# An expert layer's token weights moved to the inner rows, and an attention's keys and values projected for two groups at once

## The chip, the cores and the metric

The kernel runs on one core of a Trainium2 chip. The metric is the device time of one execution in microseconds (us); the number to compare is the median of three runs. Engines are named as in the profile: PE is TensorE, DVE is VectorE, ACT is ScalarE, POOL is GpSimd, SP is SyncE, which here only issues DMAs.

## The reference, cut to what matters

Four transformer layers follow each other, each with an attention part and an expert part. Only two of the eight parts are touched: layer 0's attention and layer 0's experts. In the kernel there are 16 batches of 256 tokens, 128 channels, all float32.

```python
# layer 0, attention: 64 query heads of 64, 8 key/value heads (each serves a group of 8 query heads)
q = (x @ Wq.T + bq); k = (x @ Wk.T + bk); v = (x @ Wv.T + bv)      # k, v repeated 8 times
allowed = (qi >= kj) & (qi - kj < 128)
logits = concat([where(allowed, q k^T * scale, -1e30), sink]); o = softmax(logits)[..., :-1] @ v
return o @ Wo.T + bo

# layer 0, experts: H = 128, M = 64, 16 experts, top 4 of 16 within the best 2 of 4 groups
scores = sigmoid(x @ gate_kernel) + gate_bias
combine = top4_weights(scores) * 2.5 / sum                          # n x 16, zero where not chosen
inter = silu(x @ w_gate[e]) * (x @ w_up[e])                         # n x 64 for each expert
y = sum_e combine[:, e] * (inter @ w_down[e])
shared = (silu(x @ sw_gate) * (x @ sw_up)) @ sw_down                # inner width 128
return y + shared
```

## The kernel before, in words

Every engine runs its own hand-written instruction stream; the streams meet in counting semaphores. `past(e, sig, v)` and `e.wait_ge(...)` are waits, `.then_inc` counts up. Parts follow each other in the order in which `program` lists them. SP loads the weights of later parts when their buffers come free.

**First attention** (`attention_plan`, `attention_pe`, `attention_dve`). The work is cut into 128 groups (16 batches times 8 key/value heads), each of two units of four query heads. A round handles unit `i`; rounds alternate even and odd. PE in each round computes `scores(i)` (L406), `values` of the unit four rounds back (L444), the transposes of the unit three rounds back (L169); an even round adds the projection step `q0` (L389) of the next group, the output projection `out` (L430) and the step `kv` of the next group (keys L382, values L384); an odd round adds `q1` (L389). The projections share one PSUM bank, `a.side`; semaphore `free` says that DVE or ACT has emptied it. For `kv` DVE runs one `tensor_scalar` for the keys (L497) and one `tensor_tensor` for the values (L500). The key weights are stored twice side by side, so that the 64 key rows of a group lie on partitions 0 to 63 and again on 64 to 127: the even heads multiply on the one half, the odd heads on the other. DVE in each round merges and masks the scores (L509, L521), writes transposed weights (L532), and computes shifts and inverses (L542 to L557). PE may write the next scores only when DVE has masked the last ones.

**First expert layer** (`moe_plan`, `moe_pe`, `moe_act`, `moe_dve`, `moe_pool`). PE computes the gate's logits during the layer norm before it. DVE then ranks the experts (`gate_groups_dve`, `rank`, L1065 to L1155) and writes `f.comb`, one weight for each token and expert. PE, ACT and DVE wait for it before the first unit. The tokens are cut into 8 blocks of 512; each block takes 9 units: 8 pairs of experts (two inner widths of 64 fill the 128 partitions) and the shared expert. In a unit PE runs two 512-column multiplications (L1205, L1207), ACT the silu (L1246), DVE the product (L1272), PE four output multiplications (L1230), and DVE multiplies the outputs by the token's weight and adds them to `f.acc` in SBUF (L1309). For a pair, the output of the two experts must stay apart, because their weights differ: the right-hand side is 256 columns wide (each half zero in the other expert's rows), and DVE runs 8 multiply-adds of 128 x 128; for the shared expert it is 128 columns and 4. At a block's end POOL multiplies by the gate row and adds to `k.X`, and DVE takes the statistics for the next layer norm. `moe_*` also serves layer 2's experts, with 16 units a block and its own code paths (`l == 2`).

Of the kernel before, what the change touches and what calls it, by code (L numbers as in the profile page):

```python
# [127 lines left out]
def setup(nc, ctx, dram, out):  # L128
# [9 lines left out]
    k.hrow = nc.dram_tensor("hrow_dram", (NB * 256, 256), F32, kind="Internal").ap()  # L138
    sb = lambda n, w: ctx.enter_context(nc.sbuf_tensor(n, [P, w], F32))
# [183 lines left out]
def attention_plan(k, l, no, w, t_w):  # L323
# [6 lines left out]
    a.qT, a.kT = R.many(2, 1024), R.many(2, 256)  # L330
    a.nv = 4
    a.va = G.many(a.nv, 128)
# [10 lines left out]
    a.uses = {("q0", 0): 0, ("kv", 0): 1, ("q1", 0): 2}  # L343
    for n in range(1, a.groups):
        for part in ("q0", "kv", "q1"):
            a.uses[part, n] = len(a.uses)
    u = a.units
    a.s = sems(k, "a", zero=2, part=2, early=u, half=3 * u, merged=2 * u, masked=3 * u, shift=u, sshift=u, exps=u, sexp=u, inv=u, norm=2 * u, turn=2 * u,
# [21 lines left out]
def attention_pe(k, a, e):  # L370
# [6 lines left out]
    def project(step, n):  # L377
# [15 lines left out]
    def scores(i):  # L393
# [3 lines left out]
        q, kt = a.qT[n % 2], a.kT[n % 2]  # L397
        e.wait_ge(*s["free"](max(taken(f"q{s4}", n), taken("kv", n))))
        past(e, s["masked"], 3 * i)
        for p, qt, j, last in ((0, 0, 0, 0), (1, 1, 0, 0), (0, 0, 1, 0), (0, 1, 0, 0), (1, 1, 1, 1), (0, 1, 1, 1),  # L400
# [5 lines left out]
            m = e.matmul(o, q[r, 256 * c + 128 * qt:256 * c + 128 * qt + 128], kt[r, 0:w_], start=True, stop=True)  # L406
# [27 lines left out]
    def values(i):  # L434
        if i is None:
            return
        v, pt = a.va[i // 2 % a.nv], a.PT[i % 2]
        past(e, s["o"], i)
        for c in range(3):
# [3 lines left out]
            for r in range(2):  # L443
                done(e.matmul(a.Ob[64 * r:64 * r + 64, at:at + 256], v[:, 64 * tile:64 * tile + 64], x[:, r],  # L444
                              start=(c != 1), stop=(c != 0)), s["values"], c == 2 and r == 1)
# [3 lines left out]
    for i, at, odd, ahead, n in attention_rounds(a):  # L449
# [14 lines left out]
        else:  # L464
# [6 lines left out]
            if ahead is not None:  # L471
                project("kv", ahead)


def attention_dve(k, a, e):
# [7 lines left out]
    e.tensor_tensor(a.isnew, k.C["ident"], k.C["tri"], ALU.add).then_inc(s["part"].sem, 1)  # L483
    c_.hold(e)
    e.wait_ge(*s["part"](2))
    e.wait_ge(*s["zero"](2))

    def project(step, n):
# [7 lines left out]
        else:  # L496
            e.tensor_scalar(a.kT[n % 2], a.side[:, 0:256], w["bk"][:, g:g + 1], None, ALU.add)  # L497
            past(e, s["values"], 2 * (n + 1 - a.nv))
            bv = w["bv"][:, 64 * g:64 * g + 64].unsqueeze(1).broadcast_to([P, 2, 64])
            e.tensor_tensor(a.va[n % a.nv].rearrange("p (t w) -> p t w", t=2),  # L500
                            a.side[:, 256:384].rearrange("p (t w) -> p t w", t=2), bv, ALU.add).then_inc(s["free"].sem, 1)
# [59 lines left out]
    for i, at, odd, ahead, n in attention_rounds(a):  # L561
# [25 lines left out]
        else:  # L587
# [6 lines left out]
            if ahead is not None:  # L594
                project("kv", ahead)
# [464 lines left out]
def rank(c, q, vals, n, C, out):  # L1060

    C4 = C.rearrange("p (t e j) -> p t e j", e=n, j=n)
    for e in range(n):
        if e:
# [3 lines left out]
                               ALU.is_gt))  # L1068
    c.hold(q)
# [19 lines left out]
def gate_groups_plan(k, f, r, spare):  # L1089
    nc_ = 17 if f.l == 0 else 16  # L1090
    f.comb = v3(r.get(NT * nc_), nc_)
    n0 = r.at
    f.g = spare.get(512), spare.get(512), r.get(128), r.get(128), r.get(512), r.get(512), r.get(32), r.get(8192)
    r.at = n0
# [7 lines left out]
def gate_groups_dve(k, f, q):  # L1102
# [35 lines left out]
    rank(c, q, m3, 16, C, rk3)  # L1138
# [14 lines left out]
    if l == 0:  # L1153
        c.then(q.memset(f.comb[:, :, 16:17], 1.0))
    q.tensor_tensor(f.comb[:, :, 0:16], w3_, bc(den, 16), ALU.mult).then_inc(f.s["comb"].sem, 1)  # L1155

# [4 lines left out]
def moe_plan(k, l, no, gate, t_w, r):  # L1161
    f = K()
    f.l, f.no, f.gate, f.t_w = l, no, gate, t_w
    f.w = views(k.W2, {0: L0F, 2: L2F}[l])
    spare = k.W2[:, width(L0F):width(L2F)] if l == 0 else k.W1[:, width(L3F):width(L1F)]
    gate_groups_plan(k, f, r, Region(spare, spare.shape[1]))
    f.sg, f.h, f.acc, f.ym = r.many(3, 512), r.many(3, 512), r.many(2, 512), r.many(2, 512)
    if l == 0:
        f.yb, f.E = [(k.bank[4], k.bank[5]), (k.bank[6], k.bank[7])], 9
    else:  # L1170
        f.yb, f.E = [(k.bank[4],), (k.bank[5],), (k.bank[6],)], 16
    f.cT = r.get(4096) if l == 2 else None
    u = 8 * f.E
    totals = dict(logits=1, gexp=1, comb=1, gated=u, lifted=u, silu=u, hidden=u, half={0: 64, 2: 8}[l], down=u,
                  sum=u + (8 if l == 2 else 0), scaled=24, tox=8)
    if l == 2:
        totals |= dict(ct=8, ctp=8)
    f.s = sems(k, "f", **totals)
# [4 lines left out]
def moe_pe(k, f, e):  # L1183
# [6 lines left out]
    if l == 2:  # L1190
        for g in range(8):
            past(e, s["ct"], g - 1)
            for j in range(4):
                done(transpose(k, e, k.bank[4 + g % 2][0:16, 128 * j:128 * j + 128], f.comb[:, 4 * g + j, :]), s["ctp"],
                     j == 3)
    for u in range(8 * E + 1):
        if u < 8 * E:
            B, x_e = divmod(u, E)
            x = k.HT[:, 512 * B:512 * B + 512]
            if l == 0 and x_e == 8:  # L1200
                w1, w3 = w["sw1"], w["sw3"]
            else:
                w1, w3 = w["w1"][:, 128 * x_e:128 * x_e + 128], w["w3"][:, 128 * x_e:128 * x_e + 128]
# [46 lines left out]
def moe_dve(k, f, e):  # L1250
# [10 lines left out]
    for u in range(8 * E + 1):  # L1261
# [11 lines left out]
        if u >= 1:  # L1273
# [11 lines left out]
            for q in range(2 if two else 1):  # L1285
                for j in range(4):
# [12 lines left out]
                    else:  # L1299
                        src = ys[0][:, 128 * j:128 * j + 128]  # L1300
                        if j == 0:
                            e.wait_ge(*s["down"](d + 1))
# [1432 lines left out]
```

## Time and profile before

| | |
|---|---|
| median of 3 runs | 4342.83 us (4336.99 to 4345.63) |
| the profiled execution's own time | 4335.0 us |
| its span, first to last instruction | 4333.2 us |
| TensorE clock granted, mean | 0.931 |
| busy: PE, DVE, ACT, POOL | 90%, 76%, 51%, 30% |
| DMA, mean over the span | 11 GB/s |
| first attention | from about 48 to 1640 us |
| first expert layer | from about 1657 to 1954 us |

Busy shares are means over stages with different limits. A busy PE is not PE at its peak: its records overlap, so what a step costs is read from the distance between the starts of neighbouring records. A float32 multiplication shows as two records, a transpose as one.

### The profile page before, as it was taken

The numbers are of one execution on the slowest core, as the hardware profiler recorded it, in microseconds if no ns is written. First come the engines' busy times: TensorE is split into PE (matmuls) and PEld (weight loads), VectorE is DVE, ScalarE is ACT, GpSimd is POOL, SyncE is SP. The second block draws the span as 40 slices with busy tenths as digits, with TensorE's granted clock in tenths as the row PEclk, the third lists the DMA queues.
The fourth block names the chain that finished last, engine by engine and source line by source line (L and its number), as shares of the span: only waits on it lengthen the run. The fifth ranks groups of instructions, "written<-read, shape, count | busy, mean of one in ns | idle before, by whom it ended". The sixth has DMA issues, their size and how long they took to land.

```text
span 4333.2 us, 78923 instructions
## 1 busy us (share of the span) xinstructions
PE 3898.3 (90%) x25405; PEld 2636.7 (61%) x25405; DVE 3302.3 (76%) x12175; ACT 2220.0 (51%) x6877; POOL 1297.2 (30%) x1077
## 2 busy tenths in 40 slices
PE   6999999999999996998998996998975999899835
PEld 5777777777777775665664443334553666555633
DVE  6888888888888886884776996776887777788561
ACT  4777777777777772114675443433222222477501
POOL 1333333333333330003453884550000000222107
PEclk9999999999999997996998998999985999999857
DMA  2000000000000002000000000000001000000103
GB/s 116 2 2 2 2 2 2 2 2 2 1 2 2 2 2 85 1 1 1 2 2 1 0 0 10 1 1 1 1 1 59 1 1 1 1 2 1 40 24 54
DMA packets 20344, 46.59 MB, mean 11 GB/s; under 512 B 1248, under 2 KB 17632, under 8 KB 18656
## 3 DMA queue, kind: packets, MB, share of 16 engines
q1 hardware_dynamic: 13792, 35.25, 2.1%
q0 software_dynamic: 6144, 6.30, 0.9%
q8 instruction: 208, 3.41, 0.3%
q14 instruction: 200, 1.64, 0.1%
HBM read 33.15 MB, written 8.39 MB: 10 GB/s over the span
## 4 chain that ended last, share of the span: by engine, by line
PE 70%; DVE 15%; issue 6%; ACT 5%; POOL 3%; DMA 1%; POOLq 0%; DVEq 0%; ACTq 0%; SPq 0%
PE ps L406 9%; PE ps L444 9%; PE ps L169 8%; PE ps L389 6%; PE ps L430 5%; PE ps L1230 5%; PE ps L1205 4%; PE ps L1207 3%; PE ps L1803 2%; PE ps L1790 2%; DVE gbbc L1842 2%; PE ps L833 2%; DVE gbbc L1837 2%; DVE gbbc L1831 2%; PE ps L797 2%
## 5 line engine op out<-in xcount | busy, mean ns | idle before, releaser
L521 DVE CUSTOM_DVE_ANT_0 T<-ps,C 128x128 f32<-128x128 f32 x2048 | 450.7, 285 | 0.0
L668 POOL TENSOR_TENSOR T<-T 128x512 f32<-128x512 f32 x256 | 260.8, 1039 | 535.2 <-DVE T L557 535.2
L668 POOL TENSOR_TENSOR W<-W,T 128x512 f32<-128x512 f32 x256 | 260.8, 1040 | 520.8 <-DVE T L557 520.8
L406 PE MATMUL ps<-T 64*128 64x128 f32 (+1 forms) x4096 | 404.7, 337 | 1.7 <-DVE T L521 1.7
L532 DVE COPY_PREDICATED W<-gbbc,ps 128x512 f32<-128x512 int32 x512 | 342.7, 722 | 82.2 <-PE ps L169 82.2
L615 ACT ACTIVATE W<-T 128x128 f32<-128x128 f32 x1024 | 396.1, 391 | 1.7 <-DVE T L542 1.7
L615 ACT ACTIVATE T<-T 128x128 f32<-128x128 f32 x1024 | 396.1, 391 | 0.5 <-DVE T L542 0.5
L444 PE MATMUL ps<-W,gbbc 128*64 128x256 f32 x3072 | 388.0, 388 | 2.7 <-ACT T L632 2.7
L406 PEld LDWEIGHTS ps<-T 64*128 64x128 f32 x4096 | 343.9, 187 | 62.9 <-issue 42.5
L169 PE MATMUL ps<-C,T 128*128 128x128 f32 (+1 forms) x1649 | 277.9, 308 | 95.0 <-DVE T L292 44.9
L169 PEld LDWEIGHTS ps<-C,T 128*128 128x128 f32 (+1 forms) x1649 | 205.5, 153 | 170.3 <-issue 63.0
L1230 PEld LDWEIGHTS ps<-W,T 128*128 128x128 f32 x1600 | 238.1, 191 | 115.8 <-issue 103.8
L1309 DVE SCALAR_TENSOR_TENSOR T<-ps,T 128x128 f32<-128x128 f32 x1024 | 286.5, 343 | 27.1 <-PE ps L1230 11.1
L389 PE MATMUL ps<-HT,W 128*128 128x256 f32 x1024 | 277.6, 394 | 2.0 <-ACT HT L315 1.1
L1230 PE MATMUL ps<-W,T 128*128 128x128 f32 (+1 forms) x1600 | 266.2, 309 | 9.0 <-DVE T L1272 5.6
L983 ACT ACTIVATE T<-ps 128x384 f32<-128x384 f32 (+1 forms) x512 | 236.0, 550 | 71.1 <-PE ps L784 71.0
L444 PEld LDWEIGHTS ps<-W,gbbc 128*64 128x64 f32 x3072 | 197.7, 136 | 108.4 <-ACT T L632 3.5
L1333 POOL TENSOR_TENSOR T<-T,gbbc 128x256 f32<-128x256 f32 x32 | 23.2, 724 | 783.5 <-DVE T L1309 783.5
L1041 POOL TENSOR_TENSOR QK<-T,QK 128x512 fp32r<-128x512 f32 x128 | 162.0, 1275 | 311.3 <-ACT T L1004 227.9
L509 DVE COPY_PREDICATED ps<-C,ps 128x256 f32<-128x256 int32 x512 | 199.3, 425 | 65.6 <-PE ps L406 65.1
L624 ACT ACTIVATE W<-ps 128x512 f32<-128x512 f32 x256 | 152.8, 597 | 186.8 <-PE ps L169 182.5
L430 PE MATMUL ps<-T,W 128*128 128x256 f32 x1024 | 242.3, 379 | 0.8 <-ACT T L632 0.8
(375 smaller groups left out, 8852.1 us busy)
## 6 DMA issues: line engine op xcount, KB each, us to landing
W<-in_l1f_dram SPq DMA_DIRECT2D x1, 6152.0 KB, 24.5
W<-in_l0a_dram SPq DMA_DIRECT2D x1, 5172.5 KB, 24.5
W<-in_l2f_dram SPq DMA_DIRECT2D x1, 3160.0 KB, 11.4
W<-in_l3f_dram SPq DMA_DIRECT2D x1, 3076.0 KB, 18.4
W<-in_sm_dram SPq DMA_DIRECT2D x1, 2729.0 KB, 9.6
W<-in_l0f_dram SPq DMA_DIRECT2D x1, 2256.0 KB, 29.4
X<-in_x_dram SPq DMA_DIRECT2D x1, 2048.0 KB, 12.7
out_dram<-X SPq DMA_DIRECT2D x1, 2048.0 KB, 8.7
```

The lines of the kernel that those rows point to most:

```text
L169: return e.transpose(out, in_, k.C["ident"])
L389: done(e.matmul(a.side[:, 256 * c:256 * c + 256], w["wq"][:, 512 * g + 128 * (2 * j + c):512 * g + 128 * (2 * j + c) + 128], x, start=True ...
L406: m = e.matmul(o, q[r, 256 * c + 128 * qt:256 * c + 128 * qt + 128], kt[r, 0:w_], start=True, stop=True)
L430: done(e.matmul(a.acc[:, 0:256], w["wo"][:, (g * a.CH + c) * 128:(g * a.CH + c + 1) * 128], a.oT[n % 2][:, 256 * c:256 * c + 256], start=( ...
L444: done(e.matmul(a.Ob[64 * r:64 * r + 64, at:at + 256], v[:, 64 * tile:64 * tile + 64], x[:, r], start=(c != 1), stop=(c != 0)), s["values" ...
L521: done(e.tensor_tensor_reduce(sm[:, at:at + 128], src, m, 1.0, -3.0e38, ALU.add, ALU.max, mx[:, col:col + 1]), s["masked"], x == (3 if ban ...
L532: e.copy_predicated(a.PT[t % 2][:, 512 * j:512 * j + 512].rearrange("p (h w) -> p h w", h=4), is_.unsqueeze(1).broadcast_to([P, 4, 128]).b ...
L615: done(e.activation(a.Pr[i % 4][:, at:at + w_], a.Sm[i % 2][:, at:at + w_], ACT.Exp, bias=a.ngs[i % 4][:, c:c + 1], scale=a.scale, accum_o ...
L668: e.tensor_tensor(pr, pr, a.rins[i % 4][:, c:c + 4].unsqueeze(2).broadcast_to([P, 4, 128]), ALU.mult).then_inc(s["norm"].sem, 1)
L983: e.activation(a.PT[n % 2][:, 512 * g:512 * g + 256 + a.w1], a.far[g][:, 0:256 + a.w1], ACT.Exp, bias=0.0, scale=a.scale).then_inc(s["exp" ...
L1230: m = e.matmul(o, hh[:, 128 * j:128 * j + 128], rhs, start=True, stop=True)
L1309: m = e.scalar_tensor_tensor(out=a, in0=src, scalar=c, in1=a, op0=ALU.mult, op1=ALU.add)
```

## The change

It has three parts, in layer 0 alone except where said.

1. **Attention, keys and values.** The `kv` step runs once for two groups. Because the key weights lie twice side by side, 128 columns taken from an offset of 64 give group g's keys on partitions 0 to 63 and group g+1's on 64 to 127. DVE adds the bias (two small copies at the part's start build `a.bk`), then copies the two halves crosswise into columns 256 to 511. The values multiplication has 128 columns where it had 64. `scores` waits for a semaphore of its own, `keys`.
2. **Experts.** New functions `fold_*` replace `moe_*` for layer 0. The token's weight multiplies the inner rows `h` before the output multiplication, and so the two experts of a pair need not stay apart: `fold_pool` adds their two zero-padded weight blocks once, the right-hand side is 128 columns wide, and all nine units of a block accumulate in one PSUM bank. The weights are needed along the columns of `h`: PE transposes `f.comb` (4 transposes for a block), ACT copies them to SBUF, SP writes them to DRAM (`crow`) and reads them back with each row broadcast over 64 partitions, two DMAs of 128 KB for a unit into one of three buffers `cB`. DVE multiplies (`scale`). The output multiplications lag five units behind (`FOLD_LAG`), and the first six units run while DVE still ranks (`between`). At a block's end DVE does what POOL did.
3. **Ranking, both expert layers with groups.** The comparison table `C` is bf16 where it was float32, in half the space. `moe_*` loses its layer 0 paths.

```diff
@@ attention_plan
+    a.qT, a.kT = R.many(2, 1024), R.many(2, 512)      # kT was 256
+    a.nv = 3                                          # was 4
+    a.va = G.many(a.nv, 256)                          # was 128
@@ attention_pe, project("kv") and scores
-            e.matmul(a.side[:, 0:256], w["wk"][:, 128 * g:128 * g + 128], x, start=True, stop=True)
+            e.matmul(a.side[:, 0:256], w["wk"][:, 128 * g + 64:128 * g + 192], x, start=True, stop=True)
             for j in range(2):
-                done(e.matmul(a.side[:, 256 + 64 * j:320 + 64 * j], x[:, 128 * j:128 * j + 128],
-                              w["wv"][:, 64 * g:64 * g + 64], start=True, stop=True), s["side"], j == 1)
+                done(e.matmul(a.side[:, 256 + 128 * j:384 + 128 * j], x[:, 128 * j:128 * j + 128],
+                              w["wv"][:, 64 * g:64 * g + 128], start=True, stop=True), s["side"], j == 1)
-        e.wait_ge(*s["free"](max(taken(f"q{s4}", n), taken("kv", n))))
+        e.wait_ge(*s["free"](taken(f"q{s4}", n)))
+        e.wait_ge(*s["keys"](n // 2 + 1))
-            if ahead is not None:
+            if ahead is not None and ahead % 2 == 0:
                 project("kv", ahead)
@@ attention_dve, project("kv")
+            c_.then(e.tensor_scalar(kt[:, 0:256], a.side[:, 0:256], a.bk[:, g // 2:g // 2 + 1], None, ALU.add))
+            past(e, s["values"], 4 * (m + 1 - a.nv))
+            e.tensor_tensor(a.va[m % a.nv]..., a.side[:, 256:512]..., bv, ALU.add).then_inc(s["free"].sem, 1)
+            c_.hold(e)
+            c_.then(e.tensor_copy(kt[0:64, 256:512], kt[64:128, 0:256]))
+            e.tensor_copy(kt[64:128, 256:512], kt[0:64, 0:256]).then_inc(s["keys"].sem, 1)
@@ rank
+        if between is not None and e % 3 == 2:
+            between()
@@ fold_rows, in SP's queue behind the load of l1f
+    put(0)                                            # waits ct(g + 1), then crow <- cT
+    put(1)
+    for B in range(8):
+        e.wait_ge(*f.d_co[B % 2](16 * (B // 2 + 1)))
+        for x in range(8):
+            u = 8 * B + x
+            past(e, f.s["scaled"], u - 2)
+            for r in range(2):
+                e.dma_start(f.cB[u % 3][64 * r:64 * r + 64, :],
+                            f.crow[2 * x + r:2 * x + r + 1, 512 * B:512 * B + 512].broadcast_to([64, 512]))...
+            if x == 5 and 1 <= B < 7:
+                put(B + 1)
@@ fold_pe
+    for u in range(72 + FOLD_LAG):
+        if u < 72:
+            past(e, s["silu"], u - 1);   e.matmul(k.bank[2 * (u % 2)][:, :], w1, x, ...)
+            past(e, s["hidden"], u - 1); e.matmul(k.bank[2 * (u % 2) + 1][:, :], w3, x, ...)
+        for g in fold_turns(u):                       # u = 5: blocks 0 and 1; u = 9 B + 7: block B + 1
+            ... wait for comb, 4 transposes ...
+        d = u - FOLD_LAG
+        if d >= 0:
+            e.wait_ge(*(s["scaled"](8 * B + x_e + 1) if x_e < 8 else s["hidden"](d + 1)))
+            for j in range(4):
+                done(e.matmul(f.acc[B % 2][:, 128 * j:128 * j + 128], hh[:, 128 * j:128 * j + 128], w2,
+                              start=(x_e == 0 and j == 0), stop=(x_e == 8 and j == 3)), s["down"], j == 3)
@@ fold_dve
+    gate_groups_dve(k, f, e, lambda: hidden(next(early)))
+    scale(0)
+    for u in range(FOLD_LAG + 1, 72 + FOLD_LAG + 2):
+        if u - FOLD_LAG < 72:
+            scale(u - FOLD_LAG)                       # waits d_cb; h = h * cB, 128 x 512, in SBUF
+        if u < 72:
+            hidden(u)                                 # waits silu, lifted; h = up * sg, 128 x 512
+        B, x_e = divmod(u - FOLD_LAG - 1, 9)
+        if x_e == 0 and B:
+            end(B - 1)                                # t = acc * gate row; X += t; 4 stats
```

## Rows read from the trace of the kernel before

**Rows 1.** The page: shares of the span of the chain that ended last, by engine.

```profile
PE 70%; DVE 15%; issue 6%; ACT 5%; POOL 3%; DMA 1%; POOLq 0%; DVEq 0%; ACTq 0%; SPq 0%
```

**Rows 2.** Busy time by window: us, busy (records) by engine, granted clock, DMA, GB/s.

```profile
900.00:1000.00 100.00, 100.00 (x766) 79.58 (x766) 81.80 (x425) 76.24 (x323) 32.60 (x32) 1.00 0.01 2
1830.00:1861.00 31.00, 30.23 (x108) 19.81 (x108) 26.01 (x85) 5.37 (x9) 2.85 (x4) 1.00 0.00 1
```

**Rows 3.** Timeline of a `kv` step and what follows on PE: start, duration, engine, line.

```profile
804.39 0.59 PE L382 MATMUL ps<-HT,W 128*128 128x256 f32 x2
...
804.82 0.55 PE L384 MATMUL ps<-W,HT 128*128 128x64 f32 x4
...
805.30 1.58 PE L406 MATMUL ps<-T 64*128 64x128 f32 x16
...
810.15 1.58 PE L406 MATMUL ps<-T 64*128 64x128 f32 x16
```

**Rows 4.** Timeline of the same group on DVE.

```profile
805.41 0.48 DVE L497 TENSOR_SCALAR T<-ps,W 128x256 f32<-128x256 f32 x1 [0.59 <-PE ps L384]
805.81 0.28 DVE L500 TENSOR_TENSOR gbbc<-ps,W 128x128 f32<-128x128 f32 x1
806.60 0.81 DVE L509 COPY_PREDICATED ps<-C,ps 128x256 f32<-128x256 int32 x2 [0.50 <-PE ps L406]
...
809.00 1.33 DVE L532 COPY_PREDICATED W<-gbbc,ps 128x512 f32<-128x512 int32 x2
```

**Rows 5.** Timeline of the ranking's end and the first units.

```profile
1683.90 8.69 DVE L1070 TENSOR_REDUCE T<-T 128x512 f32<-128x8192 f32 x1
...
1695.38 0.65 DVE L1155 TENSOR_TENSOR T<-T 128x512 f32<-128x512 f32 x1
...
1696.30 2.05 PE L1205 MATMUL ps<-HT,W 128*128 128x512 f32 x2 [29.64 <-DVE T L1155]
```

**Rows 6.** Timeline of units: a pair from 1724.97, the shared expert's outputs at 1730.13.

```profile
1724.97 1.02 PE L1205 MATMUL ps<-HT,W 128*128 128x512 f32 x2
...
1728.41 1.02 PE L1205 MATMUL ps<-HT,W 128*128 128x512 f32 x2
...
1730.13 1.05 PE L1230 MATMUL ps<-W,T 128*128 128x128 f32 x8
...
1730.38 0.69 DVE L1272 TENSOR_TENSOR T<-ps,T 128x512 f32<-128x512 f32 x1
...
1731.02 1.02 PE L1205 MATMUL ps<-HT,W 128*128 128x512 f32 x2
...
1734.05 0.29 DVE L178 BATCH_NORM_STATS2 st<-X 128x6 f32<-128x128 f32 x1 [1.70 <-POOL X L1338]
...
1945.06 2.78 PE L1230 MATMUL ps<-W,T 128*128 128x256 f32 x16
...
1953.50 0.18 DVE L180 BATCH_NORM_AGGREGATE MV<-st 128x2 f32<-128x6 f32 x1
```

**Rows 7.** The chain, in order of time: start, us, what; two block starts in succession.

```profile
1737.20 1.97 PE ps L1230 x8
...
1768.39 1.96 PE ps L1230 x8
```

**Rows 8.** Timeline of layer 2's transposes of its token weights.

```profile
3353.44 6.48 PE L169 MATMUL ps<-C,T 128*16 128x128 f32 x32 [25.91 <-DVE T L1155]
3354.56 1.46 DVE L1259 COPY T<-ps 16x512 f32<-16x512 f32 x2 [1.38 <-PE ps L169]
```

**Rows 9.** DMA issues: KB each, us from issue to landing.

```profile
W<-in_sm_dram SPq DMA_DIRECT2D x1, 2729.0 KB, 9.6
...
W<-in_eb_dram SPq DMA_DIRECT2D x1, 1024.0 KB, 4.7
```

**Rows 10.** Windows behind the expert layer, in the second attention; the granted clock is third from the end.

```profile
2000.00:2070.00 70.00, 69.84 (x458) 44.17 (x460) 31.23 (x189) 33.24 (x68) 24.01 (x21) 0.50 0.00 1
...
2090.00:2160.00 70.00, 66.34 (x773) 43.64 (x772) 53.54 (x322) 50.01 (x112) 37.02 (x32) 1.00 0.01 2
```

More of the change, by code:

```diff
@@ L593, in attention_dve @@
                 e.tensor_scalar(a.yT, a.acc[:, 0:256], w["bo"], ga, ALU.add, ALU.mult).then_inc(s["y"].sem, 1)
-            if ahead is not None:
+            if ahead is not None and ahead % 2 == 0:
                 project("kv", ahead)
@@ L1057, in bc, with rank @@
     return ap.unsqueeze(len(ap.shape)).broadcast_to(list(ap.shape) + [n])
-def rank(c, q, vals, n, C, out):
+def rank(c, q, vals, n, C, out, between=None):
     C4 = C.rearrange("p (t e j) -> p t e j", e=n, j=n)
@@ L1137, in gate_groups_dve @@
         c.hold(q)
-    rank(c, q, m3, 16, C, rk3)
+    if between is not None:
+        between()
+    rank(c, q, m3, 16, C, rk3, between)
     c.hold(q)
@@ L1152, in gate_groups_dve, with fold_plan @@
     c.hold(q)
-    if l == 0:
-        c.then(q.memset(f.comb[:, :, 16:17], 1.0))
     q.tensor_tensor(f.comb[:, :, 0:16], w3_, bc(den, 16), ALU.mult).then_inc(f.s["comb"].sem, 1)
+FOLD_LAG = 5
+def fold_plan(k, l, no, gate, t_w, r):
+    f = K()
+    f.l, f.no, f.gate, f.t_w = l, no, gate, t_w
+    f.w = views(k.W2, L0F)
+    spare = k.W2[:, width(L0F):width(L2F)]
+    n0 = r.at
+    gate_groups_plan(k, f, r, Region(spare, spare.shape[1]))
+    free = Region(r.ap[:, n0 + 512:r.at], r.at - n0 - 512)
+    f.cB, f.t, f.cT = free.many(3, 512), free.many(2, 512), free.many(2, 512)
+    f.h, f.sg = r.many(FOLD_LAG + 2, 512), r.many(2, 512)
+    f.acc, f.turn = (k.bank[4], k.bank[5]), (k.bank[6], k.bank[7])
+    f.w2 = f.w["w2"].rearrange("p (x r d) -> p x r d", x=8, r=2)
+    f.crow = k.crow
+    f.s = sems(k, "f", logits=1, gexp=1, comb=1, gated=72, lifted=72, silu=72, hidden=72, down=72, sum=8, scaled=64, ct=8,
+               ctp=8, folded=1)
+    f.d_co = [Sig(k.dsem[n], 16) for n in ("x", "l0f")]
+    f.d_cb = [Sig(k.dsem[n], 16) for n in ("const", "mods", "l0a")]
+    f.ends = (k.s_h(16 * no + 16), t_w)
+    return f
@@ new lines, in fold_act @@
+def fold_act(k, f, e):
+    s = f.s
+    gate_groups_act(k, f, e)
+    gate_rows_act(k, f.gate, e)
+    for u in range(72):
+        e.wait_ge(*s["gated"](u + 1))
+        past(e, s["hidden"], u - 1)
+        e.activation(f.sg[u % 2], k.bank[2 * (u % 2)][:, :], ACT.Silu, bias=0.0, scale=1.0).then_inc(s["silu"].sem, 1)
+        for g in fold_turns(u):
+            e.wait_ge(*s["ctp"](g + 1))
+            if g > 1:
+                e.wait_ge(*f.d_co[g % 2](16 * (g // 2)))
+            e.activation(f.cT[g % 2][0:16, :], f.turn[g % 2][0:16, :], ACT.Copy, bias=0.0,
+                         scale=1.0).then_inc(s["ct"].sem, 1)
@@ L1161, in moe_plan, with fold_pool @@
+def fold_pool(k, f, e):
+    e.wait_ge(*f.t_w)
+    e.tensor_tensor(f.w2[:, :, 0], f.w2[:, :, 0], f.w2[:, :, 1], ALU.add).then_inc(f.s["folded"].sem, 1)
 def moe_plan(k, l, no, gate, t_w, r):
@@ L1189, in moe_pe @@
     e.wait_ge(*k.s_rows(4 * f.gate.no + 4))
[L1190 to L1195, printed above, removed]
+    for g in range(8):
+        past(e, s["ct"], g - 1)
+        for j in range(4):
+            done(transpose(k, e, k.bank[4 + g % 2][0:16, 128 * j:128 * j + 128], f.comb[:, 4 * g + j, :]), s["ctp"], j == 3)
     for u in range(8 * E + 1):
@@ new lines, in moe_dve @@
+            e.wait_ge(*s["down"](d + 1))
+            for j in range(4):
+                a, src = A[:, 128 * j:128 * j + 128], f.yb[v % 3][:, 128 * j:128 * j + 128]
+                e.wait_ge(*at[j])
+                m = e.scalar_tensor_tensor(out=a, in0=src, scalar=f.comb[:, 4 * B + j, x_e:x_e + 1], in1=a, op0=ALU.mult,
+                                           op1=ALU.add)
+                if j == 3:
+                    m.then_inc(s["sum"].sem, 1)
+                    at[j] = s["sum"](v + 1)
+                else:
+                    at[j] = (c_.sem, c_.then(m))
```

225 lines of the change are left out of this document (121 added, 104 removed).

## The prediction

> **What bounds the kernel now.** I read the chain of waits first, then the windows, then the timeline of the two stages that the change touches. The chain says that PE alone carries 70% of the span [rows 1]; the windows say where. In the first attention PE is busy for the whole of a 100 us window, DVE for 81.8, ACT for 76.2; in the first expert layer PE is busy for 30.2 of 31 us, one block, and DVE for 26.0 [rows 2]. The reader is to see that both stages wait for PE and that DVE is next, with 18% and 16% of its time left. So each is priced by what the change takes from PE, and then asked whether DVE, which gets new work, becomes late.
>
> **Attention, PE.** A `kv` step begins at 804.39 and what follows it at 805.30: 0.91 us, of which the keys take 0.43 and the two values multiplications, 64 columns wide, 0.48 [rows 3]. The new step has values of 128 columns. The nearest row has eight records of that width in 0.89 us (1730.13 to 1731.02) [rows 6], so the four records of two multiplications take 0.45: no more than the 64-column ones did. At the other bound, in proportion to columns, they would take 0.96. I take 0.45, since it is the same operation and shape. 64 of 128 steps go, and the remaining 64 cost what they did: 64 x 0.91 = 58 us (27 us at the other bound).
>
> **Attention, DVE.** A group's `kv` work was 0.40 to the next start plus 0.28 [rows 4]; the new one is 0.40, a 256-column `tensor_tensor`, about 0.41 (0.28 and half the way to 0.69 [rows 4, 6]), and two copies of 64 x 256. The trace shows no such copy. With 256 columns it should lie below the 0.48 of a 256-wide operation that reads PSUM and can't be under half the 0.28 of a 128-wide one [rows 4]. I take 0.3, near the middle: together 1.4 for two groups, where it was 1.36. DVE's total doesn't grow, but all of it lies in one round. Behind it stands the merge L509, which waited 0.50 us for PE [rows 4]. Of the 0.7 us that this round gains it eats 0.5: it moves from 806.60 to about 806.85, the masks' end from 809.00 to 809.25, and PE's next scores begin at 810.15 [rows 3, 4]: 0.9 us of cover are left. If that cover went, each 0.1 us would cost 64 x 0.1 = 6 us. The new `keys` wait stands ahead of the scores' eight multiplications on PE; the copies end a whole round earlier, so I cost it at nothing, the cover being that round (4.8 us, 805.30 to 810.15). Some start-up, 1 us. **Sum for the attention: -57 us, bounds -27 to -59.**
>
> **Experts, a unit on PE.** A pair unit takes 3.44 us (1724.97 to 1728.41), the shared expert's 2.61 (1728.41 to 1731.02) [rows 6]. After the change all output multiplications have 128 columns, so every unit takes the latter: 64 x 0.83 = 53 us less.
>
> **Experts, block ends.** DVE loses the accumulations and gains one 512-wide product for each pair: about 0.6 to the next start, 0.69 alone [rows 6]. A block has 9 + 8 of these, 10.2 us, and an end of 2 x 0.72 + 4 x 0.47 = 3.3 us (two 512-wide operations that wait for each other, and four statistics of 0.29 + 0.18 [rows 6]): 13.5 of 23.5 us. But order matters. Let PE begin a unit at t. Its product `hidden` begins at t + 1.97 (1728.41 to 1730.38 [rows 6]) and frees DVE at t + 2.57. Normally `scale` follows and is done at t + 3.3, and PE wants it at t + 2.61 + 1.71 = t + 4.3: 1 us of cover. At a block's end the 3.3 us stand between: `scale` is done at t + 6.5, PE goes on at t + 6.6 and has lost 2.3 us. The four transposes of a later block fall into that hole. Seven of eight ends are of this kind: +16 us. Before, the same place cost about 31.2 - (8 x 3.44 + 2.61) = 1.05 us a block, since a block took 31.2 (1737.20 to 1768.39 [rows 7]); 8 us go. Net +8. Bounds: -8 if the hole isn't there, and +15 if semaphores add another us to each.
>
> **Experts, the beginning.** The ranking ended at 1696.03 and PE began at 1696.30 [rows 5]. Six `hidden` now stand inside it: +3.9 us (0.60 to 0.69 each). Then the weights travel before PE can multiply outputs: to the transposes 0.3 (1695.38 + 0.65 to 1696.30 [rows 5]), transposes to copy 1.1 (3353.44 to 3354.56 [rows 8]), copy 0.7 [rows 8], a DMA of 32 KB out, two of 128 KB back, `scale` 0.7. The line through two loads (1024 KB in 4.7 us, 2729 KB in 9.6 [rows 9]) has 1.8 us at no bytes and 2.9 us for 1000 KB: 1.9 out and 2.5 back. I take 2.4 and 2.8 for issue and for writes to DRAM: 8.0 us, bounds 7 and, with 4.7 for each DMA, 12. Against that, units 0 to 5 have done their two multiplications by then: 6 x 1.72 = 10.3 us of PE work (1728.41 to 1730.13 [rows 6]) off the path. The slow beginning stays, since PE idles before it as before: the first records are twice as long as later ones (2.05 against 1.02 [rows 5, 6], at 1.2 instead of 2.4 GHz). Net 3.9 + 8.0 - 10.3 = +1.6, bounds 0 to +6.
>
> One rule speaks here. The ranking's reduction reads 8192 elements in 8.69 us [rows 5]; the change makes them bf16. The Trainium skill (VectorE: DVE Perf Modes, the perf-mode tier table) says that `tensor_reduce` runs at one element a cycle whatever the type. By that rule the reduction stays at 8.69 us. The row shows float32 only and can't decide.
>
> My sum has it unchanged, since the elements are as many; the lower bound is half, 4 us in each of two layers.
>
> **Experts, the stream of DMAs.** 128 broadcasts of 128 KB. A buffer is free when its `scale` is done and wanted three pairs later, about 7.8 us less 0.7. A round trip is two DMAs at 2.5 to 4.7 us. It fits, if they overlap or not by much; SP waits for `scaled` with the writes of later blocks queued behind, due a block ahead. SP's next load, `eb`, waits far longer for another part.
>
> **Experts, the end.** From PE's last record (1945.06 + 2.78) to the last statistic (1953.50 + 0.18) 5.8 us passed [rows 6]: POOL's passes and the statistics. Now the last end takes 3.4: -2.4. POOL's one sum of the weight blocks hides in the ranking.
>
> **Sum for the experts:** -53 + 8 + 1.6 - 2.4 = -46, bounds -33 (the slow ends of the DMAs, +6, and of the block ends, +7) to -66 (no hole, half a reduction). **Together** 4335.0 - 57 - 46 = 4232 us against the profiled execution's own time. The three runs had a median 7.8 us above it; the change as a share, -2.4%, takes 4342.8 to 4240. I predict 4238 us for the median.
>
> **Rivals.**
>
> *A. Faster still, by the clock.* Behind the expert layer PE runs at 0.50 of its clock for a window of 70 us, in which it has 458 records; a like window at 1.00 has 773 [rows 10]. The work there doesn't change, but what precedes it and its timing do. Were that stretch of 70 us gone: 70 x (1 - 458/773) = 29 us less, 4209. For it: PE is as busy at the low clock (69.8 of 70) as at the high one, and it ends by itself. Against it: the execution with the profile and the three runs lie within 11 us, so it seems to come each time.
>
> *B. DVE becomes the bound in the attention.* If a copy across partitions costs 0.48 and the round's handovers another 0.9, the 0.9 us of cover go, and PE stalls by 0.3 to 0.5 in 64 groups: +20 to +30 us, 4263. For it: DVE's windows are 82% full [rows 2]. Against it: the group without `kv` gives DVE 0.7 us and all its waits back.
>
> *C. Slower: the broadcasts run one behind another.* The place is `cB`. If a DMA began only when the last had landed, a unit would need 2 x 2.2 = 4.4 us by the line through [rows 9], where PE needs 2.61: 64 x 1.8 = 115 us more, 4353, slower than before. It decides from 4.3 us a unit on. For it: 128 KB is a small transfer, and most of 2.2 us is the fixed part. Against it: SP waits only for the `scale` three pairs back, so up to three pairs of transfers may be under way, and their bytes alone, 256 KB, are 0.7 us by the same line.
>
> The Trainium skill (DMA: Bandwidth & Descriptors, rules for kernel authors) says that transfers under 64 KB pay mostly overhead and that two to disjoint partition halves serialize. By it the two halves of a pair would cost two fixed parts one behind the other, 4.4 us a unit as in C. No row here shows small ones.
>
> *D. The weights' way loses most of the stage's gain* (DMA round trips of 9 us, or a block end of 5 us): +20 us or so, 4258.
>
> **How the numbers follow.** The forecast, -80 to -120 us, has 0.68; A 0.12; B and D together 0.14; C 0.04; and 0.02 that gains and losses cancel within 0.2%, 9 us, which is about what a measurement can tell from no change. So faster 0.94, same 0.02, slower 0.04. The range takes in A's 4209, B's 4263 and the attention's other bound (30 us more, 4268), with a few us for the median's scatter: 4202 to 4270.
>
> **What would show it.** The attention should shrink from about 1592 us to 1535, with 64 steps of `kv`, PE still full, and no idle time before the scores. A pair unit should take 2.61 us and a block about 9 x 2.61 + 2.3 = 25.8, with one PE gap of about 2 us on `scale`, behind `end`. First output multiplication about 12 us behind the old end of the ranking. Wrong it would be if PE waits for `keys` or masks in each second group, if `scale` waits for a DMA in the middle of blocks, or if the clock's slow stretches lie elsewhere.

## The result, and the profile after

| | before | after |
|---|---|---|
| median beside each other | 4342.65 us | 4234.45 us (4218.75 to 4251.37, 4 runs) |
| ratio, 95% interval | | 0.9758 (0.973 to 0.9787) |
| profiled execution: own time, span | 4335.0, 4333.2 | 4251.37, 4249.6 |

The change makes the kernel 2.4% faster, 108 us by the medians; 4238 us was forecast. The sum of the stages tells less: it gives 92 us, where 103 were forecast. A stage is read here from the timeline, from the start of the first variance operation of one layer norm (L285 before, L286 after) to that of the next.

| stage, us | before | after |
|---|---|---|
| first attention | 1602.7 | 1556.6 |
| first experts | 313.2 | 267.5 |
| second attention | 363.4 | 364.7 |
| second experts and third part | 975.3 | 972.0 |
| experts of layer 2 | 422.6 | 423.4 |
| last attention | 358.1 | 365.2 |
| from the last layer norm on | 260.2 | 262.0 |

So 46.1 + 45.7 = 91.8 us are won in the two stages that the change touches. The profiled pair differs by 8 us less than that, 7 of them in the last attention, and the medians by 16 us more. Both go with the granted clock in stages whose work is unchanged: experiments 8 to 11 deal with the second, the last section with the first.

The page after: shares of the chain, then the DMA row of the token weights.

```profile
PE 70%; DVE 17%; ACT 5%; issue 4%; POOL 2%; DMA 1%; DVEq 0%; POOLq 0%; ACTq 0%; SPq 0%
...
T<-crow_dram SPq DMA_DIRECT2D x128, 128.0 KB, 2.9
```

Windows after: the same place in the attention, and 31 us of the experts.

```profile
900.00:1000.00 100.00, 100.00 (x759) 78.32 (x760) 85.56 (x435) 79.14 (x334) 33.37 (x33) 1.00 0.01 2
1714.00:1745.00 31.00, 29.10 (x134) 17.72 (x132) 17.64 (x39) 7.58 (x13) 0.00 (x0) 1.00 0.24 82
```

Against [rows 2], PE is still full in the attention with DVE at 86%, and in the experts DVE has gone from 26.0 of 31 us to 17.6 while PE has holes (stretches without work) of 2 us in all: one block end.

**Attention.** The timeline after, PE, two groups: a `kv` step from 807.88, and at 818.49 a round without one.

```profile
807.88 0.59 PE L387 MATMUL ps<-HT,W 128*128 128x256 f32 x2
808.31 0.61 PE L389 MATMUL ps<-W,HT 128*128 128x128 f32 x4
808.85 1.58 PE L413 MATMUL ps<-T 64*128 64x128 f32 x16
...
813.69 1.58 PE L413 MATMUL ps<-T 64*128 64x128 f32 x16
...
818.49 1.89 PE L437 MATMUL ps<-T,W 128*128 128x256 f32 x8
820.31 1.58 PE L413 MATMUL ps<-T 64*128 64x128 f32 x16
```

The step takes 0.97 us (0.43 + 0.54) where [rows 3] had 0.91. And without one, scores follow the output multiplication (L437) after 1.82 us. Before, a `kv` step followed it after 1.73 (802.66 to 804.39), but the trace of before has the other case too, at its end where no projection is left, and there it is 1.82 as well:

```profile
1614.19 1.89 PE L430 MATMUL ps<-T,W 128*128 128x256 f32 x8
1616.01 1.58 PE L406 MATMUL ps<-T 64*128 64x128 f32 x16
```

So two groups save 0.91 - 0.06 - 0.09 = 0.76 us, not 0.91. The distances between starts of the scores say the same: 7.44 + 7.44 before, 7.49 + 6.62 after (rounds of 4.84 or 4.85 between them in both), 0.77 less.

DVE in the same group:

```profile
808.96 0.48 DVE L511 TENSOR_SCALAR T<-ps,T 128x256 f32<-128x256 f32 x1 [0.64 <-PE ps L389]
809.36 0.41 DVE L514 TENSOR_TENSOR gbbc<-ps,W 128x256 f32<-128x256 f32 x1
809.80 0.78 DVE L517 COPY T<-T 64x256 f32<-64x256 f32 x1
810.61 0.29 DVE L518 COPY T<-T 64x256 f32<-64x256 f32 x1
810.82 0.74 DVE L526 COPY_PREDICATED ps<-C,ps 128x256 f32<-128x256 int32 x2
...
813.30 1.33 DVE L549 COPY_PREDICATED W<-gbbc,ps 128x512 f32<-128x512 int32 x2
```

The 256-column `tensor_tensor` is 0.41 as forecast, the copies are 0.78 and 0.29, not 0.3 twice. The merge begins 1.97 us behind the scores (808.85 to 810.82); before it was 1.30 [rows 3, 4]. It is 0.67 later, and still PE's next scores come at 4.84: the masks are done and DVE's next operation starts at 813.30, the scores follow at 813.69.

**Experts, beginning.** Timeline after on DVE, then on PE.

```profile
1641.92 8.69 DVE L1089 TENSOR_REDUCE T<-T 128x512 f32<-128x8192 bf16 x1
...
1653.37 0.69 DVE L1172 TENSOR_TENSOR T<-T 128x512 f32<-128x512 f32 x1
1660.90 0.69 DVE L1304 TENSOR_TENSOR T<-T 128x512 f32<-128x512 f32 x1 [6.84 <-DMA T<-crow_dram]
```

```profile
1654.11 1.87 PE L170 MATMUL ps<-C,T 128*16 128x128 f32 x8 [17.05 <-DVE T L1172]
1661.74 2.05 PE L1267 MATMUL ps<-W,T 128*128 128x128 f32 x8 [5.75 <-DVE T L1304]
...
1666.58 1.05 PE L1267 MATMUL ps<-W,T 128*128 128x128 f32 x8
...
1669.19 1.05 PE L1267 MATMUL ps<-W,T 128*128 128x128 f32 x8
```

The reduction to bf16 costs what float32 did [rows 5], 8.69 us; this agrees with the rule of the Trainium skill (VectorE: DVE Perf Modes, the perf-mode tier table) that the prediction weighed. Layer 2's ranking shows the same 8.69 us before and after. The first output multiplication stands 7.7 us behind the ranking's end (1653.37 + 0.69). Then a unit is 2.61 us.

**Experts, block end.** After, DVE and then PE.

```profile
1690.93 0.68 DVE L1312 TENSOR_TENSOR T<-ps,gbbc 128x512 f32<-128x512 f32 x1
1691.65 0.69 DVE L1314 TENSOR_TENSOR X<-X,T 128x512 f32<-128x512 f32 x1
...
1693.98 0.67 DVE L1304 TENSOR_TENSOR T<-T 128x512 f32<-128x512 f32 x1
```

```profile
1692.68 0.60 PE L170 MATMUL ps<-C,T 128*16 128x128 f32 x4
1694.71 1.16 PE L1267 MATMUL ps<-W,T 128*128 128x128 f32 x8 [1.43 <-DVE T L1304]
```

The next block's is at 1720.34: 25.63 us a block, 9 x 2.61 and a hole of 2.1.

### The profile page after: what moved, and what is told of

The parts are those of the page before. It is cut to its first block, busy times and chain, and to the rows that moved or that the text cites. A ratio compares the mean times of both kernels' runs of the same rounds, so it can differ in the third digit from the quotient of the medians.

```text
span 4249.6 us, 77674 instructions
## 1 busy us (share of the span) xinstructions
PE 3810.4 (90%) x25053; PEld 2542.4 (60%) x25053; DVE 3233.8 (76%) x11712; ACT 2228.5 (52%) x6885; POOL 1277.1 (30%) x1046
## 4 chain that ended last, share of the span: by engine, by line
PE 70%; DVE 17%; ACT 5%; issue 4%; POOL 2%; DMA 1%; DVEq 0%; POOLq 0%; ACTq 0%; SPq 0%
PE ps L413 9%; PE ps L452 9%; PE ps L170 8%; PE ps L394 6%; PE ps L437 5%; PE ps L1393 3%; PE ps L1375 2%; PE ps L1377 2%; PE ps L1940 2%; PE ps L1927 2%; DVE gbbc L1979 2%; PE ps L850 2%; PE ps L814 2%; DVE gbbc L1968 2%; DVE gbbc L1974 2%
## 5 line engine op out<-in xcount | busy, mean ns | idle before, releaser
L685 POOL TENSOR_TENSOR W<-W,T 128x512 f32<-128x512 f32 x256 | 260.8, 1039 | 525.4 <-DVE T L574 525.4
L685 POOL TENSOR_TENSOR T<-T 128x512 f32<-128x512 f32 x256 | 260.8, 1040 | 484.5 <-DVE T L574 484.5
L437 PE MATMUL ps<-T,W 128*128 128x256 f32 x1024 | 242.3, 379 | 0.8 <-ACT T L649 0.8
L1408 ACT ACTIVATE T<-ps,W 128x512 f32<-128x512 f32 x128 | 87.8, 687 | 256.9 <-PE ps L1375 256.9
L394 PEld LDWEIGHTS ps<-HT,W 128*128 128x128 f32 x1024 | 175.0, 191 | 64.6 <-issue 47.3
L170 PE MATMUL ps<-C,W 128*128 128x128 f32 x1168 | 164.8, 285 | 45.7 <-DVE W L2552 21.4
L437 PEld LDWEIGHTS ps<-T,W 128*128 128x128 f32 x1024 | 184.6, 190 | 21.0 <-issue 1.2
```

The source lines that it names most:

```text
L170: return e.transpose(out, in_, k.C["ident"])
L394: done(e.matmul(a.side[:, 256 * c:256 * c + 256], w["wq"][:, 512 * g + 128 * (2 * j + c):512 * g + 128 * (2 * j + c) + 128], x, start=True ...
L437: done(e.matmul(a.acc[:, 0:256], w["wo"][:, (g * a.CH + c) * 128:(g * a.CH + c + 1) * 128], a.oT[n % 2][:, 256 * c:256 * c + 256], start=( ...
L685: e.tensor_tensor(pr, pr, a.rins[i % 4][:, c:c + 4].unsqueeze(2).broadcast_to([P, 4, 128]), ALU.mult).then_inc(s["norm"].sem, 1)
```

## The experiments

**1 and 2. One part alone.** `x1_attention` is the kernel before with the change's three `attention_*` functions; `x2_experts` is the changed kernel with the three of before. 

> The attention's part of the change alone, the expert layer as before. From the first layer norm's start to the second's it took 1602.7 us before and 1556.6 us with the whole change. Theory: the parts are independent, so this stage takes 1556.6 us again and the expert stage its old 313 us; the total falls by 46 us, to about 4297. Rival: part of the 46 us is due to what the expert layer's change moves (another layout of the buffers), and the stage is longer than 1560 us. What lies behind the expert layer may differ by up to 30 us with the clock's slow stretches, in either direction.

> The experts' part of the change alone, attention as before. From the second layer norm's start to the third's it took 313.2 us before and 267.5 us with the whole change. Theory: 267.5 us again, the attention's 1602.7 us unchanged, total down by 46 us to about 4297. Rival: the stages behind it are what made the median fall by 108 us where the two stages give 92; then this kernel alone falls by 55 us or more, because the timing of what follows the expert layer changes here and keeps the clock high.

The first: 4295.25 us (4266.04 to 4298.74, 8 runs), ratio 0.9906 (0.9874 to 0.9939); the second 4290.23 us (4263.77 to 4301.79, 4 runs), ratio 0.99 (0.9842 to 0.9957). By stages: attention 1556.6 in the first, experts 268.5 in the second, and of the untouched stages none is more than 1.1 us shorter than before; the last attention is 5.4 and 10.1 us longer. The parts don't help or hinder each other: they give 46.1 and 44.7 us alone and 91.8 together.

**3. The copies.** The second pair of keys is written from PSUM with the bias, not copied:

```diff
+ c_.then(e.tensor_scalar(kt[0:64, 256:512], a.side[64:128, 0:256], a.bk[64:128, ...], None, ALU.add))
+ e.tensor_scalar(kt[64:128, 256:512], a.side[0:64, 0:256], a.bk[0:64, ...], None, ALU.add).then_inc(s["keys"].sem, 1)
- c_.then(e.tensor_copy(kt[0:64, 256:512], kt[64:128, 0:256]))
- e.tensor_copy(kt[64:128, 256:512], kt[0:64, 0:256]).then_inc(s["keys"].sem, 1)
```

> The two crosswise copies of the keys, which read SBUF, become two tensor_scalar that read PSUM (with the bias), ahead of the values' operation. The first copy took 0.78 us in the median where the second took 0.29. Theory: the first copy waits for POOL, which multiplies at that time; operations that read PSUM take 0.4 to 0.5 us each whatever POOL does, with no outliers, and since PE never waited for them the attention stays at 1556.6 us within 1 us. Rival: the missing 9 us of the attention (46 measured, 57 forecast) hang on that wait; then the stage falls by 4 us or more.

One run, 4225.55 us; attention 1557.0, as in the changed kernel. Its DVE timeline:

```profile
809.46 0.49 DVE L512 TENSOR_SCALAR T<-ps,T 64x256 f32<-64x256 f32 x1
809.98 0.48 DVE L513 TENSOR_SCALAR T<-ps,T 64x256 f32<-64x256 f32 x1
810.49 0.42 DVE L517 TENSOR_TENSOR gbbc<-ps,W 128x256 f32<-128x256 f32 x1
810.83 0.75 DVE L526 COPY_PREDICATED ps<-C,ps 128x256 f32<-128x256 int32 x2
```

The attention doesn't fall by 4 us, so the rival goes. But the merge starts as late as with the copies (810.83 and 810.82), since the two operations take 0.97 us where the copies took 1.07: the run takes away the wait for POOL and doesn't show what a lighter DVE would give. That PE sees neither is in the distances between its scores, which are those of the changed kernel. Where the 0.78 us come from is under the unexpected, below.

**4. The block end.** In `fold_dve`, the next `scale` ahead of `end`, not behind it:

```diff
+ B, x_e = divmod(u - FOLD_LAG - 1, 9)                        # stood behind hidden(u)
- if u - FOLD_LAG < 72:
+ if u - FOLD_LAG < 72 and (x_e != 1 or B == 0):
      scale(u - FOLD_LAG)
...
  if x_e == 0 and B:
+     if B < 8:
+         scale(u + 1 - FOLD_LAG)
      end(B - 1)
```

> At a block's end DVE does the next pair's scale before the end's seven operations instead of behind them. PE's gap of 1.43 us behind seven blocks closes. Theory (the hole comes from the order on DVE): a block takes 23.5 to 24.2 us instead of 25.63, the expert stage 267.5 - 7 x 1.4 = 257.5 us. Rival (DVE as a whole is too slow there, or the broadcast for the earlier scale isn't there yet): the gap moves to the next unit and the stage gains under 3 us.

One run, 4218.13 us; expert stage 258.0 where it was 267.5. DVE, then PE:

```profile
1691.18 0.68 DVE L1304 TENSOR_TENSOR T<-T 128x512 f32<-128x512 f32 x1
1691.78 0.68 DVE L1312 TENSOR_TENSOR T<-ps,gbbc 128x512 f32<-128x512 f32 x1
```

```profile
1692.92 0.60 PE L170 MATMUL ps<-C,T 128*16 128x128 f32 x4
1693.36 1.06 PE L1267 MATMUL ps<-W,T 128*128 128x128 f32 x8
```

Output multiplications hardly wait here: the three distances at a block's end are 3.05, 2.82 and 2.72 instead of 4.64, 2.72 and 2.61, and 0.44 us of the first are the four transposes. A block takes 24.25 us where it took 25.63. The wait came from the order on DVE.

**5. One buffer for the weights.**

```diff
- f.cB, f.t, f.cT = free.many(3, 512), ...      past(e, f.s["scaled"], u - 2)
+ f.cB, f.t, f.cT = free.many(1, 512), ...      past(e, f.s["scaled"], u)       # u % 3 becomes u % 1
```

> One buffer for the token weights where the changed kernel has three; all else the same. Each unit's two transfers then wait for the multiply of the unit before (issue, 2.9 us from issue to landing, 0.7 us multiply). Theory (the transfers are hidden only because three buffers let them run two units ahead): a routed unit takes 4.2 to 4.6 us where it took 2.61, so 64 units lose 1.6 to 2.0 us each less the cover of the shared-expert unit: the expert stage, 267.5 us between the second and third layer norm, becomes 370 to 395 us, and scale names the DMA as releaser in each unit. Rival (the transfers would land in time anyway, since DVE is idle 1 us of each unit): the stage grows by less than 20 us.

One run, 4320.59 us; expert stage 343.3, 75.8 us more. DVE in the middle of a block:

```profile
1707.53 0.69 DVE L1304 TENSOR_TENSOR T<-T 128x512 f32<-128x512 f32 x1 [2.82 <-DMA T<-crow_dram]
1708.14 0.68 DVE L1294 TENSOR_TENSOR T<-ps,T 128x512 f32<-128x512 f32 x1
...
1711.72 0.69 DVE L1304 TENSOR_TENSOR T<-T 128x512 f32<-128x512 f32 x1 [2.90 <-DMA T<-crow_dram]
```

A unit takes 4.1 to 4.2 us in the middle of a block and up to 4.9. The mechanism is as expected and its sum too high: after each shared-expert unit, which needs no weight, three units come 2.6 to 3.9 us apart. This is what rival C would have been: at 4.2 us a unit, near its threshold of 4.3, the experts take 30 us more than before the change, and 25 us of the change's gain are left.

From the end of one `scale` (1708.22) to the landing of both halves (1711.72) pass 3.5 us, where one DMA takes 2.9 from issue to landing; one behind the other they would take 5.8. The rule of the Trainium skill (DMA: Bandwidth & Descriptors, rules for kernel authors) that transfers to disjoint halves serialize isn't borne out here in their fixed part; of their bytes, a small part of the 2.9 us, this row says nothing.

**6. No early units.** The six `hidden` behind the ranking instead of inside it (`gate_groups_dve(k, f, e)`, then the loop). 

> The six hidden rows that DVE writes between the steps of the ranking are written after it instead, behind the reduction to the weights; all else as in the changed kernel. Theory (PE's first units then run behind the ranking's end, and the transposes stand behind units 2 to 5 on PE's queue, so that the round trip by way of DRAM starts later): first output multiply 14 to 18 us behind the end of the ranking where it was 7.7, the expert stage 267.5 becomes 274 to 278 us. Rival (the round trip of 7.7 us would cover the six units): the stage stays within 2 us of 267.5.

One run, 4235.64 us; expert stage 273.9, 6.4 more. PE there, the ranking having ended at 1650.73:

```profile
1660.33 1.04 PE L170 MATMUL ps<-C,T 128*16 128x128 f32 x8
1667.54 2.04 PE L1267 MATMUL ps<-W,T 128*128 128x128 f32 x8 [6.17 <-DVE T L1304]
```

16.8 us behind the ranking: the transposes queue behind the units and the transfers start that much later.

**7. The `keys` wait in one round of four.**

```diff
+ if i % 4 == 0:
      e.wait_ge(*s["keys"](n // 2 + 1))
```

> In the attention TensorE waits for the semaphore of the copied keys only in the first of the four rounds that use them, instead of in every round. The changed kernel's saving is 0.77 us per two groups where 0.91 was forecast, with 0.05 in the wider values, 0.09 in a bubble ahead of the scores. Theory (the bubble comes from the added wait instruction): the scores follow the output matmul 0.05 to 0.1 sooner in three rounds of four, and the attention, 1556.6 us from first to second layer norm, becomes 1546 to 1552. Rival (waiting for a semaphore that is already past costs nothing here, and the bubble is the change of operands): 1556 to 1557.

One run, 4250.01 us; attention 1554.8. But the distances between scores are those of the changed kernel to 0.01 us (4.84, 7.49, 4.85, 6.62, again and again), and the 1.8 us lie ahead of the first of them: scores begin 16.7 us behind the stage's start, in two traces of the unedited changed kernel 18.8 and 17.5. My theory fell: a wait that is already satisfied costs nothing here, and the 0.09 us are what scores pay behind an output multiplication, as the row of before at 1616.01 shows.

**8. The edits together,** 3, 4 and 7. 

> The changed kernel with three edits: the second half of the keys is written from PSUM in place of the two copies, the block's end stands behind the next multiply on DVE, and TensorE waits for the keys once in four rounds. Theory: attention as in the run that tries the last edit alone, expert stage 258 us, so some 10 us below the changed kernel in the same kind of second attention: median 4215 to 4228 beside 4234, spans near 4207 where the second attention takes 337 us and near 4235 where it takes 364. Rival (what the experts give comes back in a longer second attention): within 3 us of the changed kernel.

4237.71 us (4233.6 to 4246.66, 5 runs), ratio 0.9774 (0.974 to 0.9807): not below the changed kernel. The expert stage is 258.7, so the 10 us were won, but the second attention took 372.0 us in the profile, as the rival had it. That led to the clock.

**9 to 11. The clock in the second attention.** Eleven traces with this attention's work unchanged fall in two kinds: 363.4 to 372.0 us (before, after, the changed kernel again, and experiments 1, 2, 5, 7, 8) or 336.5 to 337.8 (3, 4 and 6). I call them the long and the short kind. Windows, after, a long one:

```profile
1890.00:1990.00 100.00, 97.55 (x568) 59.50 (x570) 46.38 (x284) 41.54 (x84) 31.26 (x26) 0.52 0.00 1
```

in experiment 8, the longest:

```profile
1887.00:1999.00 112.00, 110.62 (x664) 67.72 (x663) 51.34 (x309) 46.92 (x97) 34.63 (x29) 0.50 0.00 1
```

and in experiment 3, a short one:

```profile
1896.00:1916.00 20.00, 18.91 (x50) 10.46 (x50) 8.95 (x59) 3.99 (x8) 2.60 (x3) 0.51 0.00 0
1916.00:1996.00 80.00, 76.23 (x865) 50.20 (x865) 59.07 (x357) 58.31 (x125) 43.60 (x37) 0.99 0.01 2
```

The granted clock, third from the end, stays at half (1.2 of 2.4 GHz) for some 100 us with PE busy for nearly all of them, or for 20. In the first of the three windows it is back for 3 us in between.

`x11_again` is the changed kernel, unedited. 

> The changed kernel itself, unedited, five more times, since its four times (4218.8, 4225.0, 4243.9, 4251.4) lie further apart than the gain of 10 us that the edit of the block end should bring. Theory (the scatter is the second attention's two kinds of clock stretch, 337 and 364 us): times fall in two bunches, about 4218 to 4226 and 4243 to 4252. Rival (a scatter of another origin): they fill the space between. By the stages alone the change is worth 92 us in either kind.

4250.24 us, six times: 4215.1, 4215.6, 4249.5, 4251.0, 4251.0, 4252.9; ratio 0.9763 (0.9728 to 0.9799). Two bunches 34 us apart. The kernel before has them too: of 31 times in three comparisons 9 lie at 4313 to 4318 us and 22 at 4335 to 4348. The mean granted clock of each execution splits them in the same way: 0.936 to 0.938 in the lower bunch of either kernel, 0.927 to 0.933 in the upper. Bunch against bunch, the change gives 98 us (4316 to 4218) or 91 (4342 to 4251); the 92 of the stages are in line. The medians' 108 hold some 10 to 17 us of the draw: all four executions of before were in the upper bunch, and two of the four after in the lower. What isn't shown: no lower execution of an unedited kernel left a trace, and the two kinds of second attention are 27 us apart, the bunches 34.

`x10_warm`, on top of 8, and `x12_warm2`, on top of 4, add idle multiplications (128x512, outputs unused) ahead of the second attention's first scores:

```diff
- yield "warm", 4 if s == -6 else 1
+ yield "warm", 4                                             # x10_warm
+ yield "warm", 4 if s == -6 else 2 if a.causal else 1       # x12_warm2
```

> As x9_best, and ahead of the second attention's first scores TensorE runs four idle matmuls of 128x512 at each of eight more places where it ran one (24 more, outputs unused). In the changed kernel this attention shows a granted clock of 0.50 for some 90 us in one kind of execution (364 us for the stage) and for 16 us in the other (337 us). Theory (TensorE's load just before decides): all executions are of the fast kind, less up to 14 us for the 24 matmuls of 0.59 us, so times agree within 5 us and lie near 4210 to 4222. Rival (the kind is not set by this load): both kinds appear again, some 27 us apart, and the median is 0 to 14 us above x9_best.

> The changed kernel with the block end behind the next multiply, and with two idle matmuls where there was one at eight places ahead of the second attention's first scores (8 more of 0.59 us; the run before had 24 more, there and in the fourth layer, which cost 17 us in the fourth and left all five times within 4 us). Theory (a fuller TensorE there keeps the long stretch at 0.50 out): second attention near 342 us in each run, times 4208 to 4222 all told. Rival (8 are too few): two bunches, 4212 to 4216 and 4238 to 4242, and a median above 4230.

`x10_warm`: 4255.41 us (4254.58 to 4258.25, 5 runs), ratio 0.982. The spread is gone, as the theory said, and the second attention takes 363.5 us with a low stretch of 38: 26 us more than in the short kind, of which the added work is 24 x 0.59 = 14. The median lies 33 us above what was expected at most. The price of the added work was mis-sized, since the same steps serve the last attention too (364.6 to 381.6 us there) and the 14 us fall due twice. `x12_warm2`: 4221.3 us (4217.1 to 4228.48, 5 runs), ratio 0.9729 (0.9706 to 0.9752). Second attention 347.5. Its windows:

```profile
1882.00:1918.00 36.00, 32.69 (x188) 19.25 (x187) 19.55 (x129) 15.28 (x28) 11.51 (x10) 0.95 0.00 1
1918.00:1946.00 28.00, 27.53 (x206) 17.65 (x205) 14.40 (x81) 12.80 (x28) 10.21 (x9) 0.52 0.01 1
```

A low stretch of 28 us is left, later than before. None of these ten executions is of the long kind, by its mean granted clock (0.935 to 0.938), where without the added work 11 of 15 were (0.927 to 0.931; the changed kernel 6 of its 10, experiment 8 all 5). So what PE does just ahead has a part in it. `x12_warm2` is the version to keep: 29 us below the changed kernel's median in the same comparison. How much of that the eight added multiplications give isn't measured, since experiment 4 without them was run once (4218.13 us, of the short kind); against the short kind they cost 11 us (347.5 and 336.5). By the intervals of the ratios the two still touch, since the changed kernel's own two kinds make its wide.

## Why the prediction was right, and where it was not

- **Attention, -57 forecast, -46.1 measured, inside the bounds.** The mis-sized term is "64 x 0.91 = 58": it is 62 x 0.77 = 48, since the first and the last pair of groups don't show the pattern. Two causes: "so the four records of two multiplications take 0.45", from a row of eight records, measured 0.54; and a handover of 0.09 us from output multiplication to scores which I had not priced, though it stood in the trace. From first to last scores the stage is 47.3 us shorter (1560.6 to 1513.3). Ahead of the first it is 1.2 longer (17.6 to 18.8 us; 1 was forecast), but that is no price of the change: the same kernel again took 17.5 there, and 1555.9 for the stage.
- **Attention, DVE.** "It eats 0.5 [...] 0.9 us of cover are left": the copies took 1.07, not 0.6, and the merge came 0.67 later relative to the scores where 0.25 was forecast. Of the cover (the time by which DVE is done before PE needs it) 0.39 us were left, not 0.9 (813.30 to 813.69). It held: the scores wait for DVE three times in the whole stage, 4.2 us in all. DVE is busy for 85.6 of 100 us where it was 81.8, mostly because 3% more groups pass in them. No stall on `keys`. Rival B did not come about, but was nearer than it seemed.
- **Experts, a unit: 64 x 0.83.** 2.61 us, as forecast.
- **Block ends, 25.8 forecast, 25.63 measured.** The hole of 2.3 is 2.1, and 4 shows the cause of 1.4 of them; 0.44 are the transposes.
- **Beginning, +1.6 forecast, about +1.1.** The ranking ended 3.7 us later (3.9 forecast), and the weights travelled 7.7 (8.0 forecast); the 10.3 that go off are the forecast's own, which no row measures alone. Without the early units the stage takes 6.4 us more (6). "First output multiplication about 12 us behind the old end" stands: 3.7 + 7.7 = 11.4. The reduction was unchanged.
- **DMA stream.** Free in the middle of blocks: all `scale` waits on DMAs in 198 us add to 3.5 us. PE waited for them in the last units (1.4 us ahead of its last two), which I had not seen.
- **End, -2.4 forecast.** PE's last record to the next layer norm: 5.9 us before, 3.2 after, -2.7.
- **Experts together, -46 forecast, -45.7 measured.** Here the mechanism and the sum both hold: from PE's first unit behind the ranking (after: its first output multiplication) to its last record the stage shrank by 54 us, 11 came on ahead of that and 2.7 went behind it. Rivals C and D did not come about; 5 shows what three buffers are worth, 76 us.
- **Rival A.** Its counter, "it seems to come each time", was wrong: three runs and a profile all of the long kind hid a short one, which the kernel before shows in 9 of 31 times. It is no gain of the change, since both kernels have both kinds. The forecast of 4238 lies between the two bunches, so it met the median of 4234 partly by luck: 11 us too much from the attention, and a draw in which two of four runs were short, which brought about as much back.

## What to carry to other kernels

Price a step by the distance between starts, and look in the trace of before for the very neighbours that the edit will make; the end of a loop often shows them already. When a product is moved ahead of a multiplication, look at what stands in front of it in the vector engine's order at block ends: here one swap in that order gave 10 us more. And before an edit worth 10 us is judged, repeat the unedited kernel until its kinds are known.

## What was not expected of the hardware

**A copy that waits for POOL.** Of the 128 copies L517 and L518, 64 took 0.29 us and 64 took 0.54 to 1.03, nearly all 0.78. The slow ones are exactly those that began while POOL ran L685 (here 808.40 to 810.44), and each ended 0.15 us behind the end of POOL's operation:

```profile
808.40 2.04 POOL L685 TENSOR_TENSOR T<-T 128x512 f32<-128x512 f32 x2 [4.17 <-DVE T L574]
```

The same rows written from PSUM (3) take 0.48 to 0.49 each time. The Trainium skill (SBUF — State Buffer, Who interferes with whom) says that a copy in a two-port mode and a GpSimd operation take turns by an exclusive lock; the counts and the 0.15 us agree. It cost nothing here. On a critical path the copy that meets POOL (0.78) would lose to the one read from PSUM (0.48), the copy that doesn't (0.29) would win.

**The clock.** In the second attention it stays at half for 68 to 113 us without a break, with PE busy, in one kind of execution, and for 10 to 20 in the other, with that stage's work the same. With more work just ahead the stretch is 28 and 38 us in the one trace of each, and comes later. What decides between the kinds in an unedited kernel stays open.

The last attention has its own scatter, 356.8 to 368.2 us in the traces without added work in it. Its records are the same in number, and its time goes with the granted clock; before, then after:

```profile
3715.00:4073.00 358.00, 328.00 (x3208) 200.99 (x3208) 284.71 (x657) 240.10 (x451) 83.64 (x70) 0.96 0.01 2
3622.40:3987.60 365.20, 335.45 (x3208) 205.14 (x3208) 285.48 (x658) 240.45 (x451) 83.73 (x70) 0.94 0.01 1
```

Added up, the clock is at half for 30 us of it before and 44 after. The two traces with the least (26 and 30 us) have the shortest stage (356.8 in experiment 5, 358.1 before), the two with the most (53 and 54) the longest (367.0 in the changed kernel again, 368.2 in experiment 2). So the 7 us that the profiled pair loses there are a matter of the clock and not of added work. Whether the change makes the low clock likelier there isn't shown: before has one trace.
